# Adaptive-norm, attention and feed-forward block on one core: another order for TensorE's condition products and ScalarE's copies in the last steps

## The reference

```
h   = w1[idx1] applied to x (mixes the 64 tokens of a batch) + bias[idx1]
x1  = x + Wo . softmax(q k^T / sqrt(32) + alibi, causal) v     16 heads of 32
g   = w2[idx2] applied to x1 (mixes the 64 tokens of a batch)
up  = quant8(fwht(g)) . ternary(w_up)^T                        512 -> 1024
r   = relu(up)^2
y   = x1 + quant8(fwht(r)) . ternary(w_down)^T                 1024 -> 512
```

## Time and profile before

| what | value |
|---|---|
| median of 3 runs | 760.96 us (759.18 to 761.47) |
| the profiled execution's own time | 757.46 us |
| its span, first to last instruction | 755.7 us |
| TensorE busy | 730.3 us, 97% |
| VectorE busy | 666.3 us, 88% |
| ScalarE busy | 421.3 us, 56% |
| GpSimd busy | 207.9 us, 28% |
| mean granted TensorE clock | 0.998 of full |
| `cond2_turned`, 3 calls of 128 records | 4.92 us each on the chain that ended last |

### The profile page before, as it was taken

One profiled execution on the slowest core, in us unless ns is written; L12 is line 12 of the kernel. 1 busy time (PEld: TensorE's weight loads), 2 busy tenths in 40 slices (PEclk: granted clock), 3 DMA queues, 4 the chain that ended last, 5 costly groups with the idle time before them and its releaser, 6 DMA issues.

```text
span 755.7 us, 23734 instructions
## 1 busy us (share of the span) xinstructions
PE 730.3 (97%) x9936; PEld 619.6 (82%) x9936; DVE 666.3 (88%) x1346; ACT 421.3 (56%) x842; POOL 207.9 (28%) x223
## 2 busy tenths in 40 slices
PE   7888999999999999999999999999999999999897
PEld 4777888888888888888888888888888888887673
DVE  3696999999999999999999999999999999887877
ACT  2568556556565565565655655656556555573331
POOL 1123333222333332223333332233333322231100
PEclk9999999999999999999999999999999999999999
DMA  7651111001111110111111101111111110000000
GB/s 240 226 183 37 37 50 47 23 34 51 49 51 51 51 48 22 35 48 51 51 50 50 46 25 34 50 50 51 51 51 49 33 32 29 18 18 2 30 30 28
DMA packets 37568, 39.94 MB, mean 53 GB/s; under 512 B 21205, under 2 KB 21589, under 8 KB 37461
## 3 DMA queue, kind: packets, MB, share of 16 engines
q1 hardware_dynamic: 34324, 32.04, 13.7%
q10 hardware_dynamic: 3136, 6.39, 2.3%
HBM read 30.02 MB, written 8.39 MB: 51 GB/s over the span
## 4 chain that ended last, share of the span: by engine, by line
PE 84%; DVE 7%; ACT 3%; DMA 3%; POOL 1%; issue 1%; SPq 1%; ACTq 0%; DVEq 0%
PE bank L390 43%; PE bank L541 7%; PE bank L582 7%; PE bank L523 4%; PE bank L380 4%; PE bank L550 4%; PE bank L416 4%; PE bank L462 3%; PE bank L479 3%; PE bank L513 2%; DMA v_kd<-in_L_attn_Wv_dram 2%; POOL gT L282 1%; PE bank L531 1%; PE bank L566 1%; DMA late<-in_L_ffn_w_down_dram 1%
## 5 line engine op out<-in xcount | busy, mean ns | idle before, releaser
L282 POOL TENSOR_TENSOR gT<-gT 128x256 f32<-128x256 f32 x116 | 98.3, 868 | 426.0 <-ACT gT L795 423.7
L282 DVE TENSOR_TENSOR hid<-hid 128x512 f32<-128x512 f32 (+1 forms) x130 | 98.6, 799 | 0.2
L770 ACT ACTIVATE v_kd<-bank 64x256 f32<-64x256 f32 x128 | 48.6, 380 | 71.0 <-PE bank L390 69.9
L390 PE MATMUL bank<-h_hi,wk_hi 128*128 128x256 f32 x252 | 74.2, 294 | 5.8 <-ACT kT L759 5.8
L1395 POOL TENSOR_TENSOR s<-s,srow 128x512 f32<-128x512 f32 x64 | 67.5, 1059 | 41.0 <-DVE srow L1014 41.0
L390 PE MATMUL bank<-h_hi,wq_hi 128*128 128x256 f32 x256 | 74.6, 292 | 0.0
L390 PE MATMUL bank<-h_hi,wq_lo 128*128 128x256 f32 x256 | 72.2, 282 | 0.0
L390 PE MATMUL bank<-h_lo,wq_hi 128*128 128x256 f32 x256 | 72.2, 282 | 0.0
L390 PE MATMUL bank<-h_lo,wk_hi 128*128 128x256 f32 x252 | 71.6, 284 | 0.0
L390 PE MATMUL bank<-h_hi,wk_lo 128*128 128x256 f32 x252 | 71.6, 284 | 0.0
L806 ACT ACTIVATE late<-bank 128x512 f32<-128x512 f32 x64 | 37.6, 588 | 51.3 <-PE bank L541 51.2
(11 more groups left out here) (146 smaller groups left out, 1970.1 us busy)
## 6 DMA issues: line engine op xcount, KB each, us to landing
x_in<-in_x_dram SPq DMA_DIRECT2D x32, 256.0 KB, 2.6
x_res<-in_x_dram SPq DMA_DIRECT2D x32, 256.0 KB, 3.4
out_dram<-late SPq DMA_DIRECT2D x31, 256.0 KB, 3.4
w_in<-in_L_cond_weights_dram SPq DMA_DIRECT2D x126, 16.0 KB, 2.4
bias_in<-in_fside_8xS_dram SPq DMA_DIRECT2D x62, 32.0 KB, 3.2
k_bd<-in_L_attn_Wk_dram ACTq DMA_DIRECT2D x1, 1024.0 KB, 5.3
s<-in_L_attn_Wq_dram ACTq DMA_DIRECT2D x1, 1024.0 KB, 7.9
v_kd<-in_L_attn_Wv_dram ACTq DMA_DIRECT2D x1, 1024.0 KB, 12.2
```

The lines of the kernel that those rows point to most:

```text
L282: eng.tensor_tensor(dv[:, :, n], sv[:, :, 0], sv[:, :, 1], op).then_inc(done, 1)
L390: mm = pe.matmul(dst, lhs(a, k), rhs(b, k), start=(k == 0 and n == 0), stop=(k == KC - 1 and n == 2))
L770: ins = act.activation(v_kd[b * T:b * T + T, c % 4, e], blocks[e * T:e * T + T, :, b, :], ACT.Copy)
```

## The change

Four edits, all in the last steps; the number of instructions stays the same on every engine.

1. `cond2_turned`: the loop over m goes outside those over e and f. The same 64 products, with the same operands and the same accumulation for each output, now take the four quadrants in turn.
2. TensorE calls `cond2_turned(29)` ahead of `turn_p(30, 0)` and no longer between `turn_p(30, 0)` and `turn_p(30, 1)`.
3. ScalarE calls `copy_v(31)` and `copy_o(30)` ahead of `exp(31, 0)` and `exp(31, 1)`.
4. The odd blocks of pair 31 go to `gT2`, which nothing uses by then, and the wait for `clip2(30)` goes.

```
+        def odd_of(f):
+            return (gT2 if f == LAST else hid_odd)[:]
...
                 for n in range(KC):
-                    for e in range(2):
-                        r = slice(e * T, e * T + T)
-                        for f in range(2):
-                            for m in range(KC):
-                                sign = ((m & n) ^ ((m & n) >> 1)) & 1
+                    for m in range(KC):
+                        sign = ((m & n) ^ ((m & n) >> 1)) & 1
+                        for e in range(2):
+                            r = slice(e * T, e * T + T)
+                            for f in range(2):
                                 x0 = m * P + f * T
                                 mm = pe.matmul(dst[f * T:f * T + T, e, n, :], ...,
                                                start=(m == 0), stop=(m == KC - 1))
...
             v_product(30)
+            cond2_turned(29)
             turn_p(30, 0)
-            cond2_turned(29)
             turn_p(30, 1)
...
                 act.wait_ge(s_f2, 2 * f + half + 1)
-                if f == LAST:
-                    act.wait_ge(d_q2t, LAST)
...
-                act.activation(hid_odd[:, 2 * half:2 * half + 2, :], odd, ACT.Copy).then_inc(a_odd, 1)
+                act.activation(odd_of(f)[:, 2 * half:2 * half + 2, :], odd, ACT.Copy).then_inc(a_odd, 1)
...
             scale_y1(29)
+            copy_v(31)
+            copy_o(30)
             exp(31, 0)
             exp(31, 1)
-            copy_v(31)
-            copy_o(30)
             squares(29)
...
-                    dve.tensor_tensor(dst[:, :, n], even, hid_odd[:, 2 * half:2 * half + 2, :], op).then_inc(d_fly, 1)
+                    dve.tensor_tensor(dst[:, :, n], even, odd_of(f)[:, 2 * half:2 * half + 2, :], op).then_inc(d_fly, 1)
```

## The result

The changed kernel took 755.23 us (median of 5 runs, 753.31 to 756.51) beside 759.81 for the kernel before on the same chip (5 runs, 759.18 to 761.47): a ratio of 0.994, interval 0.9924 to 0.9956, so 4.6 us faster. The forecast was 754.8 in a range of 752.6 to 757.8, from a gain of 6.2. The time came out inside the range, but the gain is 1.6 us smaller than forecast: as the experiments show, the edits gave 6.7 us, and TensorE's clock took part of it back.

What follows compares the result with a forecast made beforehand. Three cond2_turned calls on the chain (14.8 us) were the costly piece, with VectorE's idle brackets capping the win; 0.9 + 1.5 + 1.85 + 1.65 + 0.3 = 6.2 us off 760.96 gave 754.8 us, range 752.6 to 757.8.

Steps and rivals of the forecast that it cites:

- The cost of a call: Each cond2_turned call, 128 records, falls from 4.92 to 2.1 us, judged by condition's same quadrant order.
- the bound from above: A cond2_turned call stays at 4.92 us if accumulation sets the old pace; as a rival 759.1 us, 7%.
- The page's rule: Rival at cond2_turned: about half the weight loads stay exposed, 3.5 us a call, gain 5.5, time 755.5; 8%.
- The new bound: Behind cond2_turned(30) and (31), max1 starts when VectorE's col_max ends, so 1.85 and 1.65 us are gained.
- the bounds of 3.1 and 3.9: Longest cond2_turned call that still costs the path nothing: 3.9 us at pair 29, 3.1 at pair 30.
- The sum at full clock: Gains over the last steps added: 0.9 + 1.5 + 1.85 + 1.65 + 0.3 = 6.2 us.
- ScalarE's order: Copies ahead of pair 31's exponentials let down(27) follow up(29) without waiting for V; 1.5 us gained.
- the odd copy: Pair 31's odd-block copy no longer waits for clip2(30), so VectorE's fly0 starts sooner; 0.3 us gained.
- edit 2, costed together with edit 1 at pair 29: Shorter, earlier cond2_turned(29) lets turn_max(28) start behind col_max(28) and max2(28) at 687.9, not 688.80; 0.9 us.
- The clock: the step that failed: Rival: TensorE's longer thin stretch between hadamard1(30) and turn_q1(30) halves its clock; at most 1.7 us more, 756.5; 10%.
- The place I named: Thin stretch between hadamard1(30) and turn_q1(30), clock falling at 712; some 3.4 us of following products take twice their time.

Runs made afterwards that it cites:

- the runs on the pace: Two kernels, each the changed one with fillers, its three cond2_turned calls each in a different product order, some without sums; one execution each, 753.33 and 753.66 us.
- fillers: Changed kernel plus 17 products with unused results in TensorE's idle time, at four places; 752.76 us beside 759.42 for the kernel before, ratio 0.9904.
- the second group of fillers alone: Changed kernel plus only the 11 products with unused results between turn_p(31,0) and turn_q1(30); 752.48 us, ratio 0.9911 to the kernel before.

## Why the prediction was right, and where it was not

- *The cost of a call.* Forecast 2.1 us, from a row of another function with the same quadrant order. Measured 2.00 to 2.02. Accumulation as the cause of the old pace, which was the bound from above, is excluded: 4.97 us without sums.
- *The page's rule.* By the Trainium skill ("TensorE: Matmul & The Clock Gate", Part 3) only a change of row group lets a weight load overlap; by my estimate from it a call would have taken 3.5 us. The call with only the column half alternating took 2.74, as little as with rows: here the rule doesn't hold, for 64 x 64 float32 products.
- *The new bound.* Forecast: VectorE, with `max1` right behind `col_max`, twice. So it is, and the calls of 2.7 us in the runs on the pace, below the bounds of 3.1 and 3.9, changed nothing.
- *The sum at full clock.* 6.2 us forecast, 6.69 measured with fillers. At `add_out(27)` the shift was 2.68 and not 2.4: `up(29)` started 1.08 us earlier, not 0.9, and `down(27)` followed 1.80 us behind it, not 1.89 (from the changed kernel's trace; the profile with fillers lacks the first record of `down(27)`). The rest came in steps of 0.1 us at each `max1`, where I had subtracted rows that overlap a little.
- *ScalarE's order and the odd copy.* 1.5 and 0.3 us forecast; 1.58 and 0.28 in the profiles. For edit 2, costed together with edit 1 at pair 29, the runs show that its own share is nothing.
- *The clock: the step that failed.* I gave it 10%, one place, at most 1.7 us. In both profiled executions of the changed kernel it fell in two places and cost 3.3 us. The place I named came about as priced: at `up(30)` the clock was low for some 6.9 us and not 3.4, but TensorE was idle in part of that, and it cost 1.83 us. The other place, 1.50 us, I left out though its cause stood in my own sum: I had TensorE through with the transposes at 685.8 us and waiting for `col_max(28)` to 687.5.
- *The total.* That 754.8 forecast and 755.23 measured agree so well is in part luck. The forecast took 6.2 us off a median of 760.96 from three runs; with five it is 759.81, and the gain was 4.6. The profiled execution was forecast at 751.3 and took 755.54: 1.45 us because `fly0(28)`, ahead of all edits, came later, and 3.33 for the clock, less the 0.5 by which the edits gave more. That the two low places explain the missing gain is shown by the fillers, with which the rows in them run at full clock and the whole 6.69 us is there.

It stays open how often each stretch falls in unprofiled executions; only their mean clock is known. The kernel before may lose time to the clock as well: of its 38 executions beside the experiments the ten with a mean clock of 0.989 to 0.991 took 760.60 to 761.63 us, and all others 757.40 to 759.78. The one that was profiled had 0.998 and no low stretch behind 672 us, so differences of medians and of profiles need not agree.

## What to carry to other kernels

Order small products so that neighbours use different quadrants of the array: 38 ns a record became 16 with no other change, and the accumulation order inside each output stayed. When TensorE's work shrinks in a stretch where another engine sets the pace, look at what its idle time does to its clock, and fill it if products on the path follow. Read each gain off the idle bracket that it closes: those of 1.85 and 1.65 us gave 1.94 and 1.76, and that of 1.33, in which one transposition has to stay, 0.91; the 14.8 us of busy time, shrunk by 8.7, say nothing of the size.

## What the runs showed of the hardware that was not expected

A change of only the column half overlaps as well as a change of only the row half (2.74 and 2.68 us for 128 records, against 4.97 in one quadrant and 2.02 in four). The granted clock fell to 0.50 with no idle time longer than 1.75 us ahead of it: TensorE had transposes, a few 128 x 128 products and waits in between. Before the change a stretch with 0.98 us of work in 3.40 kept its clock, and with the second group of fillers alone the same instructions and the same 1.75 us of waiting ahead of `scores(31)` kept it too. So how thin a stretch is does not by itself say whether it falls.
